# A macaron block of FFN, retention and FFN in fp32: how the first FFN prepares its weights and its x tiles, and in which order its engines work

## The chip, the core and the metric

The kernel runs on one core of a Trainium2 chip, in one launch. The metric is the device time of that launch in microseconds (us). The engines are called as in the profile: PE is TensorE, PEld its weight loads, DVE VectorE, ACT ScalarE, POOL GpSimd, SP the engine that only issues transfers (SPq).

## The reference

x has 1024 rows of 256 values, all in fp32. Both FFNs have the same weights.

```python
def ffn(x):      # scales are per output column; w_fp8 = w.astype(float8_e4m3fn).astype(float32)
    gate = silu((x @ gate_w_fp8) * gate_scale)          # 256 -> 768
    up = (x @ up_w_fp8) * up_scale                      # 256 -> 768
    return ((gate * up) @ down_w_fp8) * down_scale      # 768 -> 256
x = x + 0.5 * ffn(layernorm(x))
x = x + attn(layernorm(x))   # 16 heads of 16, rotated q and k, decay mask, group norm, silu gate, projection
x = x + 0.5 * ffn(layernorm(x))
```

## The kernel before

The rows of x are 8 tiles of 128 (NT), in two groups of four (NG, TH). Nothing is scheduled by a tool: each engine has a list of calls written out by hand, and executes it strictly in that order; semaphores with counts tie the lists together. A call that waits holds up all that stands behind it in its own list.

**Weights.** The first FFN rounds them to the fp8 grid itself. They come in eight pieces (PIECES): gate and up columns 0 to 127 (pieces 0, 1), 128 to 383 (2, 3), 384 to 767 (4, 5), and two halves of down (6, 7), with 256, 512, 768, 768 values a partition. For each piece DVE does `grid_step` (L574, exponent bits out of the raw weights), `grid_clip` (L580) and `grid_add` (L586, raw weight plus grid value); then the grid value is subtracted again, which leaves the rounded weight: `subtract`, on POOL (L293) for the pieces in SUB_ON_POOL, on DVE (L592) for the others. ACT copies the result twice: `to_half` (L385) to fp16 with a scale, `to_weights` (L391) to the fp32r tile that PE reads.

**x tiles.** For each tile `tile_stats` (L603) and `mean_var` (L607) on DVE, `roots` on POOL (L300, L302: 1/sqrt of the variances of a whole group of tiles), `norm_tile` on DVE (L632). PE turns each tile (`turn_h`, L961) into the banks of `turn`; when all four tiles of a group are turned, ACT copies the high halves (`split_h`, L398) and DVE takes the rest (`rest_h`, L644). So every product is done with a high and a low half.

**Products.** PRODUCTS lists twelve pairs (g, i) of the first FFN: group g, 128 columns i. `gate_up(j)` (L986) is 8 matmuls of 512 columns: gate high, gate low, up high, up low, two each. ACT does `silu` (L408), DVE `fuse_up` (L660), ACT `split_f` (L416), and the rest of it, `rest_f`, is on POOL (L308) for REST_ON_POOL, on DVE (L668) for the others. Product j shares its two banks with j-2. `down` (L1014) makes one x tile out of six column blocks; `scale_down` (L678) on DVE and `add_down` on POOL (L314) or, in the second FFN, on DVE (L683), add it to x. `turn_h2` (L1030) hands the first tile to the attention part.

**PE's filler.** WARM_UP matmuls on zeros (L1170) stand at the start, and `keep_busy` (L943) calls between the first steps.

**Transfers.** SP issues all of them, in the order gate piece 0, x tiles 0 to 3, up piece 1, gate piece 2, the masks, four small rows, x tiles 4 to 7, up piece 3, pieces 4 to 7, and then what later parts need.

## Time and profile before

| | us |
|---|---|
| median of 3 runs | 173.49 (173.36 to 173.67) |
| the profiled execution, its own time | 173.6 |
| its span, first to last instruction | 171.8 |
| PE busy | 161.0 (94%) |
| DVE busy | 137.1 (80%) |
| ACT busy | 75.9 (44%) |
| POOL busy | 68.9 (40%) |

PE is busy in 94% of the span, by a model that lets pipelined matmuls overlap, and it also counts the matmuls on zeros. Between the span and the time of the execution lie 1.8 us outside the instructions. The granted clock of TensorE is given as 0.999.

### The profile page before, as it was taken

The numbers are of one execution on the slowest core, as the hardware profiler recorded it, in microseconds if no ns is written. First come the engines' busy times: TensorE is split into PE (matmuls) and PEld (weight loads), VectorE is DVE, ScalarE is ACT, GpSimd is POOL, SyncE is SP. The second block draws the span as 40 slices with busy tenths as digits, with TensorE's granted clock in tenths as the row PEclk, the third lists the DMA queues.
The fourth block names the chain that finished last, engine by engine and source line by source line (L and its number), as shares of the span: only waits on it lengthen the run. The fifth ranks groups of instructions, "written<-read, shape, count | busy, mean of one in ns | idle before, by whom it ended". The sixth has DMA issues, their size and how long they took to land.

```text
span 171.8 us, 3264 instructions
## 1 busy us (share of the span) xinstructions
PE 161.0 (94%) x1125; PEld 123.1 (72%) x1125; DVE 137.1 (80%) x294; ACT 75.9 (44%) x162; POOL 68.9 (40%) x76
## 2 busy tenths in 40 slices
PE   5996998989989999999999999999899999999992
PEld 2454766678969786768686777867666788898881
DVE  2799989999847266869797979998887899666763
ACT  3145398869402306161707062534716646225600
POOL 2354295425580611117474746465297530000000
PEclk9999999999999999999999999999999999999999
DMA  4999203803000000000000000000000000011002
GB/s 155 277 352 310 84 2 64 306 0 120 4 0 0 4 0 0 4 0 0 6 0 4 2 0 0 4 0 6 0 0 2 0 4 0 0 61 61 6 31 92
DMA packets 6848, 8.41 MB, mean 49 GB/s; under 512 B 416, under 2 KB 5552, under 8 KB 6832
## 3 DMA queue, kind: packets, MB, share of 16 engines
q1 hardware_dynamic: 6832, 8.20, 14.9%
q8 instruction: 9, 0.15, 0.4%
q14 instruction: 7, 0.06, 0.1%
HBM read 7.15 MB, written 1.05 MB: 48 GB/s over the span
## 4 chain that ended last, share of the span: by engine, by line
PE 62%; DVE 19%; issue 7%; POOL 6%; DMA 3%; ACT 2%; SPq 0%; POOLq 0%; DVEq 0%
PE bank L986 18%; PE bank L1014 10%; PE bank L1042 7%; PE bank L1107 5%; POOL grstd L324 3%; PE bank L1053 3%; PE bank L1085 3%; PE bank L1056 3%; PE bank L1163 3%; DVE h L632 3%; DMA xt<-in_L_attn_x 3%; PE bank L1068 2%; DVE fuse L660 2%; DVE sc L715 2%; DVE grid L574 2%
## 5 line engine op out<-in xcount | busy, mean ns | idle before, releaser
L986 PE MATMUL bank<-hh,gate_r 128*128 128x512 f32 x96 | 27.6, 407 | 2.5 <-DVE hh L644 1.0
L986 PE MATMUL bank<-hh,up_r 128*128 128x512 f32 x96 | 26.3, 396 | 0.0
L1014 PE MATMUL bank<-down_r,fhi 128*128 128x256 f32 x96 | 24.3, 291 | 0.3 <-DVE flo L668 0.3
L324 POOL TENSOR_TENSOR grstd<-gve,neg_half 128x16 f32<-128x16 f32 x8 | 23.3, 2917 | 0.7
L1014 PE MATMUL bank<-down_r,flo 128*128 128x256 f32 x96 | 23.4, 282 | 0.0
L408 ACT ACTIVATE gact<-bank,vec 128x512 f32<-128x512 f32 x24 | 16.4, 685 | 14.9 <-PE bank L986 14.6
L986 PEld LDWEIGHTS bank<-hh,gate_r 128*128 128x128 f32 x96 | 16.8, 188 | 8.0 <-issue 3.7
L660 DVE SCALAR_TENSOR_TENSOR fuse<-bank,vec,gact 128x512 f32<-128x512 f32 x24 | 17.9, 745 | 4.1 <-PE bank L986 3.9
L986 PEld LDWEIGHTS bank<-hh,up_r 128*128 128x128 f32 x96 | 18.1, 188 | 4.3
L715 DVE TENSOR_TENSOR sc<-bank,msk 128x512 f32<-128x512 f32 x32 | 19.8, 680 | 0.0
L433 ACT ACTIVATE v<-bank 128x256 f32<-128x256 f32 x8 | 3.1, 384 | 37.0 <-PE bank L1056 37.0
L1014 PEld LDWEIGHTS bank<-down_r,fhi 128*128 128x128 f32 x96 | 18.1, 188 | 1.5 <-DVE flo L668 1.0
L1014 PEld LDWEIGHTS bank<-down_r,flo 128*128 128x128 f32 x96 | 18.1, 188 | 0.5 <-issue 0.2
L416 ACT ACTIVATE fhi<-fuse 128x512 fp32r<-128x512 f32 x24 | 14.9, 629 | 6.8 <-DVE fuse L660 6.8
L1042 PE MATMUL bank<-wqkv,h 128*128 128x512 f32 x32 | 15.1, 594 | 0.0
L668 DVE TENSOR_TENSOR flo<-fuse,fhi 128x512 fp32r<-128x512 f32 x18 | 13.3, 744 | 0.8 <-ACT fhi L416 0.7
L678 DVE TENSOR_TENSOR yd<-bank,ds 128x256 f32<-128x256 f32 x16 | 6.7, 422 | 8.5 <-PE bank L1014 8.4
L1107 PE MATMUL bank<-sc,v 128*32 128x128 f32 x256 | 13.1, 279 | 0.0
L300 POOL TENSOR_SCALAR ve<-mv 128x1 f32<-128x1 f32 (+3 forms) x14 | 3.8, 272 | 23.0 <-DVE mv L607 22.9
L293 POOL TENSOR_TENSOR grid<-raw,grid 128x256 f32<-128x256 f32 (+2 forms) x6 | 7.7, 1290 | 12.3 <-DVE raw L586 12.3
L308 POOL TENSOR_TENSOR flo<-fuse,fhi 128x512 fp32r<-128x512 f32 x6 | 9.6, 1611 | 4.9 <-ACT fhi L416 4.9
L302 POOL TENSOR_TENSOR rstd<-ve,neg_half 128x1 f32<-128x1 f32 (+3 forms) x14 | 10.0, 715 | 1.2
(80 smaller groups left out, 300.0 us busy)
## 6 DMA issues: line engine op xcount, KB each, us to landing
raw<-in_rotation SPq DMA_DIRECT2D x1, 1536.0 KB, 7.1
xt<-in_L_attn_x SPq DMA_DIRECT2D x2, 512.0 KB, 5.4
out<-xt SPq DMA_DIRECT2D x8, 128.0 KB, 1.7
raw<-in_L_ffn_down_w SPq DMA_DIRECT2D x2, 384.0 KB, 8.2
wqkv<-in_L_attn_w_qkv SPq DMA_DIRECT2D x1, 768.0 KB, 9.6
raw<-in_rotation SPq DMA_DIRECT2D x1, 512.0 KB, 3.5
raw<-in_L_ffn_gate_w SPq DMA_DIRECT2D x1, 384.0 KB, 7.2
raw<-in_L_ffn_up_w SPq DMA_DIRECT2D x1, 384.0 KB, 7.7
```

The lines of the kernel that those rows point to most:

```text
L302: pool.tensor_tensor(rstd[:, a:b], ve[:, a:b], neg_half[:, 0:b - a], ALU.pow).then_inc(rstd_done, 1)
L308: pool.tensor_tensor(flo[:, g % NG, i, :], fuse[:, j % FUSE_SLOTS, :], fhi[:, g % NG, i, :].bitcast(F32), ALU.subtract).then_inc(flo_pool, 1)
L324: pool.tensor_tensor(grstd[:, c % 2], gve[:, :], neg_half[:, :], ALU.pow).then_inc(grstd_done, 1)
L408: nc.scalar.activation(gact[:, j % 2, :], pairs[j // (NG * NI)][j % 2][0][:, :], ACT.Silu, scale=gate_col[:, i:i + 1]).then_inc(silu_done, 1)
L416: nc.scalar.activation(fhi[:, g % NG, i, :], fuse[:, j % FUSE_SLOTS, :], ACT.Copy).then_inc(fhi_done, 1)
L660: dve.scalar_tensor_tensor(out=fuse[:, j % FUSE_SLOTS, :], in0=pairs[j // (NG * NI)][j % 2][1][:, :], scalar=up_col[:, i:i + 1], in1=gact[ ...
L668: dve.tensor_tensor(flo[:, g % NG, i, :], fuse[:, j % FUSE_SLOTS, :], fhi[:, g % NG, i, :].bitcast(F32), ALU.subtract).then_inc(flo_dve, 1)
L715: dve.tensor_tensor(sc[:, r].rearrange("p k m t -> p (k m) t"), b_sc[r][:, :].rearrange("p (g t) -> p g t", t=P), causal.unsqueeze(1).to_b ...
L986: mm = pe.matmul(dst[:, :], wr[m][:, k * I + i * P:k * I + (i + 1) * P], half[:, k, g % NG, :], start=(k == 0 and half is hhi), stop=(k == ...
L1014: mm = pe.matmul(downs[d][:, 0:C], half[:, g % NG, i, t * P:(t + 1) * P], wr["down"][:, i * C:(i + 1) * C], start=(i == 0 and half is fhi) ...
L1042: mm = pe.matmul(b_qk[:, :], h2[:, c % 2, k, :], wqkv[:, k, 0:2 * C], start=(k == 0), stop=(k == KC - 1))
L1107: mm = pe.matmul(b_y[r * 2 * D:(r + 1) * 2 * D, k * P:(k + 1) * P], v2[:, c % 2, hd, :], sc[:, r, k, m, :], start=(c == 0 and m == 0), sto ...
```

## The change

Weights: there is one ACT pass instead of two (`to_weights` reads the grid tile in fp32, with the scale), the fp16 tile is gone, and the grid tile has three slots instead of two. The scale of the grid (LIFT) goes into `grid_clip` as a second operation, and `grid_add` becomes a plain addition. The new scales of h, of the weights and of the fused product cancel in the vectors and in `half_scale`.

x: it comes in three transfers (tiles 0 and 1, 2 and 3, 4 to 7), the first one ahead of all others. The roots of the first FFN are taken in three groups (0, 1), (2, 3), (4 to 7). Tiles 0, 2, 4 and 6 are normalised by ACT (`norm_act`), which needs a small DVE operation per group (`shift_rows`), tiles 1, 3, 5 and 7 by DVE as before.

PE: the first product does both high halves before both low halves (`first_gate_up`); the gate parts of products 1 and 2 come ahead of `turn_h(1)`, the up parts behind it; in `gate_up` the gate part waits for one thing (the silu of j-2) and the up part for the other (the fuse of j-2), in both FFNs. WARM_UP goes from 5 to 3, the `keep_busy` calls from 9 to 4. The last `down` calls of the second FFN stand in another order: the last two column blocks come only after the first four of tiles 4 to 6, and tile 7 is done whole at the end.

The lists of all engines in the first FFN are new, the sharing of `subtract` and `rest_f` between DVE and POOL too. The diff, cut to its core (indented less; lists as far as they change):

```diff
-GRID = 2.0 ** -20
+LIFT = 2.0 ** 20
 GRID_MIN = 1.5 * 2.0 ** -6
-W_SCALE = 144.0
+W_SCALE = 1.125 * 2.0 ** 119
+H_SCALE = 2.0 ** -90
+F_SCALE = 2.0 ** -60
+GRID_SLOTS = 3
+X_ROOTS = 3
...
-SUB_ON_POOL = [0, 1, 2, 3, 4, 6]
+SUB_ON_POOL = [1, 2, 3, 4, 5, 7]
...
-REST_ON_POOL = [0, 1, 2, 6, 8, 11]
+REST_ON_POOL = [0, 1, 2, 4, 11]
 FUSE_SLOTS = 4
-WARM_UP = 5
+WARM_UP = 3
...
+def normed_until(n):
+    return (n + 1) // 2 if n < NT else n + 1 - NT // 2
...
+        root_groups = ([(0, 2), (2, TH), (TH, NT)] + [(n, n + 1) for n in range(NT, 2 * NT)]
...
+sp.dma_start(xt[:, 0:2, :], x_dram[0][:, 0:2, :]).then_inc(x_in[0], 16)
 load_piece(0)
-sp.dma_start(xt[:, 0:TH, :], x_dram[0]).then_inc(x_in[0], 16)
+sp.dma_start(xt[:, 2:TH, :], x_dram[0][:, 2:TH, :]).then_inc(x_in[1], 16)
 load_piece(1)
-load_piece(2)
 sp.dma_start(msk[:, :], mask_t).then_inc(mask_in, 16)
 for src, at, n in ((gate_s, 0, NI), (up_s, NI, NI), (gn_w, 2 * NI, KC), (gn_b, 2 * NI + KC, KC)):
     sp.dma_start(rows[at:at + n, :], src.rearrange("(i p) -> i p", p=P)).then_inc(rows_in, 16)
-sp.dma_start(xt[:, TH:NT, :], x_dram[1]).then_inc(x_in[1], 16)
-for q in range(3, len(PIECES)):
+load_piece(2)
+load_piece(3)
+sp.dma_start(xt[:, TH:NT, :], x_dram[1]).then_inc(x_in[2], 16)
+for q in range(4, len(PIECES)):
     load_piece(q)
...
 pool.wait_ge(const_done, 1)
-subtract(0)
 roots(0)
-for n in range(1, 4):
-    subtract(n)
 roots(1)
+subtract(1)
+subtract(2)
+subtract(3)
+roots(2)
 subtract(4)
-for n in range(0, 3):
-    rest_f(n)
-subtract(6)
-rest_f(6)
-rest_f(8)
+rest_f(0)
+subtract(5)
+rest_f(1)
+rest_f(2)
+rest_f(4)
+subtract(7)
 add_down(0)
+roots(X_ROOTS)
 add_down(1)
-rest_f(11)
+roots(X_ROOTS + 1)
 add_down(2)
 add_down(3)
-roots(3)
-roots(4)
-for n in range(4, 8):
-    add_down(n)
+rest_f(11)
+roots(X_ROOTS + 2)
+add_down(4)
+add_down(5)
+add_down(6)
+add_down(7)
...
-def to_half(q):
+def to_weights(q):
     if q in SUB_ON_POOL:
         act.wait_ge(sub_pool, subs(q + 1)[1])
     else:
         act.wait_ge(sub_dve, subs(q + 1)[0])
-    if q >= 2:
-        act.wait_ge(w_ready, q - 1)
-    nc.scalar.activation(packed(w16, q), packed(grid, q), ACT.Copy,
-                         scale=W_SCALE / GRID).then_inc(half_done, 1)
-def to_weights(q):
-    act.wait_ge(half_done, q + 1)
-    nc.scalar.activation(piece(wr[PIECES[q][0]][:, :], q), packed(w16, q), ACT.Copy).then_inc(w_ready, 1)
+    nc.scalar.activation(piece(wr[PIECES[q][0]][:, :], q), packed(grid, q), ACT.Copy,
+                         scale=W_SCALE).then_inc(w_ready, 1)
+def norm_act(n):
+    act.wait_ge(shift_done, roots_until(n))
+    if n >= TH:
+        act.wait_ge(turned, n - TH + 1)
+    nc.scalar.activation(h[:, n % TH, :], xt[:, n, :], ACT.Identity, scale=rstd[:, n:n + 1],
+                         bias=shift[:, n:n + 1]).then_inc(h_act, 1)
...
+    nc.scalar.activation(hhi[:, k, g % NG, :], turn[g][k][:, :], ACT.Copy, scale=H_SCALE).then_inc(hhi_done, 1)
...
 nc.scalar.activation(warm[:, :], neg_half[:, 0:1], ACT.Silu)
-to_half(0)
+norm_act(0)
 to_weights(0)
-to_half(1)
-to_weights(1)
-to_half(2)
+norm_act(2)
 split_h(0, 0)
 split_h(0, 1)
+to_weights(1)
 to_weights(2)
-to_half(3)
+silu(0)
 to_weights(3)
-silu(0)
+norm_act(4)
+norm_act(6)
 silu(1)
 split_h(1, 0)
 split_h(1, 1)
 split_f(0)
 silu(2)
+to_weights(4)
+silu(3)
+silu(4)
 split_f(1)
-to_half(4)
-silu(3)
-to_weights(4)
 split_f(2)
-to_half(5)
-silu(4)
+split_f(3)
 to_weights(5)
 silu(5)
-split_f(3)
+silu(6)
 split_f(4)
-silu(6)
 split_f(5)
-to_half(6)
 silu(7)
 to_weights(6)
+split_f(6)
+split_f(7)
 silu(8)
-for n in range(6, 9):
-    split_f(n)
 silu(9)
-to_half(7)
+split_f(8)
 to_weights(7)
 silu(10)
 split_f(9)
+silu(11)
+copy_h2(0)
 split_f(10)
-silu(11)
 split_f(11)
-copy_h2(0)
-copy_v(0)
 copy_h2(1)
 copy_qk(0)
+copy_v(0)
 for c in range(NT - 1):
...
     dve.wait_ge(raw_in[q], 16)
-    if q >= 2:
-        dve.wait_ge(half_done, q - 1)
+    if q >= GRID_SLOTS:
+        dve.wait_ge(w_ready, q - GRID_SLOTS + 1)
...
-    dve.tensor_scalar(packed(grid, q), packed(grid, q), GRID_MIN, None, ALU.max).then_inc(clip_done, 1)
+    dve.tensor_scalar(packed(grid, q), packed(grid, q), GRID_MIN, LIFT, ALU.max, ALU.mult).then_inc(clip_done, 1)
-    dve.scalar_tensor_tensor(out=w, in0=w, scalar=GRID, in1=packed(grid, q),
-                             op0=ALU.mult, op1=ALU.add).then_inc(added, 1)
+    dve.tensor_tensor(w, w, packed(grid, q), ALU.add).then_inc(added, 1)
...
+def shift_rows(g):
+    a, b = root_groups[g]
+    dve.wait_ge(rstd_done, g + 1)
+    dve.scalar_tensor_tensor(out=shift[:, a:b], in0=mv[:, a:b, 0], scalar=-1.0, in1=rstd[:, a:b],
+                             op0=ALU.mult, op1=ALU.mult).then_inc(shift_done, 1)
...
-    dve.tensor_scalar(vec[:, 0:2 * NI], bank[7][:, 0:2 * NI], 1.0 / W_SCALE, None, ALU.mult).then_inc(vec_done, 1)
+    dve.tensor_scalar(vec[:, 0:NI], bank[7][:, 0:NI], 1.0 / (W_SCALE * H_SCALE), None,
+                      ALU.mult).then_inc(vec_done, 1)
+    dve.tensor_scalar(vec[:, NI:2 * NI], bank[7][:, NI:2 * NI], F_SCALE / (W_SCALE * H_SCALE), None,
+                      ALU.mult).then_inc(vec_done, 1)
...
-    dve.tensor_tensor(hlo[:, k, g % NG, :], turn[g][k][:, :], hhi[:, k, g % NG, :].bitcast(F32),
-                      ALU.subtract).then_inc(hlo_done, 1)
+    dve.scalar_tensor_tensor(out=hlo[:, k, g % NG, :], in0=turn[g][k][:, :], scalar=H_SCALE,
+                             in1=hhi[:, k, g % NG, :].bitcast(F32), op0=ALU.mult,
+                             op1=ALU.subtract).then_inc(hlo_done, 1)
...
+tile_stats(0)
 grid_step(0)
-grid_clip(0)
-grid_add(0)
-tile_stats(0)
 tile_stats(1)
 mean_var(0)
+grid_clip(0)
+mean_var(1)
+grid_add(0)
 tile_stats(2)
-mean_var(1)
 tile_stats(3)
+grid_step(1)
 mean_var(2)
-grid_step(1)
 mean_var(3)
+shift_rows(0)
+grid_clip(1)
+norm_tile(1)
+subtract(0)
 grid_step(2)
-grid_clip(1)
+norm_tile(3)
 grid_clip(2)
+grid_step(3)
+shift_rows(1)
+grid_clip(3)
 grid_add(1)
 grid_add(2)
-for n in range(0, 4):
-    norm_tile(n)
+grid_add(3)
+rest_h(0, 0)
 tile_stats(4)
+rest_h(0, 1)
+mean_var(4)
+tile_stats(5)
+tile_stats(6)
+tile_stats(7)
+mean_var(5)
+mean_var(6)
+mean_var(7)
 turned_vectors()
-mean_var(4)
-grid_step(3)
-tile_stats(5)
-grid_clip(3)
-rest_h(0, 0)
-grid_add(3)
-tile_stats(6)
-mean_var(5)
-tile_stats(7)
-mean_var(6)
 grid_step(4)
-mean_var(7)
-rest_h(0, 1)
+grid_step(5)
 grid_clip(4)
-grid_step(5)
-for n in range(4, 8):
-    norm_tile(n)
+shift_rows(2)
+norm_tile(5)
+norm_tile(7)
+grid_add(4)
+grid_clip(5)
 fuse_up(0)
-grid_clip(5)
-grid_add(4)
 rest_h(1, 0)
+rest_h(1, 1)
 fuse_up(1)
-rest_h(1, 1)
+fuse_up(2)
+grid_step(6)
 grid_add(5)
-fuse_up(2)
-subtract(5)
+grid_clip(6)
 fuse_up(3)
-grid_step(6)
-half_scale()
-grid_clip(6)
 fuse_up(4)
 grid_add(6)
+rest_f(3)
 fuse_up(5)
+subtract(6)
+fuse_up(6)
+fuse_up(7)
 grid_step(7)
-rest_f(3)
-fuse_up(6)
 grid_clip(7)
-rest_f(4)
+grid_add(7)
 rest_f(5)
-fuse_up(7)
-grid_add(7)
 fuse_up(8)
-subtract(7)
+rest_f(6)
 rest_f(7)
+rest_f(8)
+half_scale()
+scale_down(0)
 fuse_up(9)
 fuse_up(10)
+tile_stats(NT)
+scale_down(1)
 rest_f(9)
-scale_down(0)
+mean_var(NT)
+scale_down(2)
+norm_tile(NT)
+tile_stats(NT + 1)
+mean_var(NT + 1)
+scale_down(3)
+norm_tile(NT + 1)
+fuse_up(11)
 rest_f(10)
-scale_down(1)
-tile_stats(8)
-fuse_up(11)
-mean_var(8)
-tile_stats(9)
-scale_down(2)
-mean_var(9)
-norm_tile(8)
-scale_down(3)
+tile_stats(NT + 2)
+mean_var(NT + 2)
 rotate_parts(0)
-norm_tile(9)
 rotate(0)
-tile_stats(NT + 2)
...
     for t in range(TH):
-        if g == 0 and t == 1:
+        if g == 0 and t >= 2:
             keep_busy(1)
-        pe.wait_ge(h_done, n0 + t + 1)
+        if g < NG and t % 2 == 0:
+            pe.wait_ge(h_act, g * TH // 2 + t // 2 + 1)
+        else:
+            pe.wait_ge(h_done, normed_until(n0 + t))
         for k in range(KC):
             mm = pe.transpose(turn[g][k][:, t * P:(t + 1) * P], h[:, (n0 + t) % TH, k * P:(k + 1) * P], ident)
         mm.then_inc(turned, 1)
+def first_gate_up():
+    pe.wait_ge(hhi_done, KC)
+    for half in (hhi, hlo):
+        if half is hlo:
+            pe.wait_ge(hlo_done, KC)
+        for m in ("gate", "up"):
+            pe.wait_ge(w_ready, 1 if m == "gate" else PIECES_NEEDED[0])
+            for k in range(KC):
+                mm = pe.matmul(pairs[0][0][m == "up"][:, :], wr[m][:, k * I:k * I + P], half[:, k, 0, :],
+                               start=(k == 0 and half is hhi), stop=(k == KC - 1 and half is hlo))
+            if half is hlo:
+                mm.then_inc(gate_done if m == "gate" else up_done, 1)
 def gate_up(j, parts=("gate", "up")):
...
-    if g < NG:
-        pe.wait_ge(w_ready, PIECES_NEEDED[i])
     if i == 0:
         pe.wait_ge(hhi_done, KC * (g + 1))
-    if j >= 2:
-        pe.wait_ge(silu_done, j - 1)
-        pe.wait_ge(fuse_done, j - 1)
     if j == NG * NI:
         pe.wait_ge(hlo_done, KC * (NG + 1))
     elif j == NG * NI + 1:
         pe.wait_ge(sc_masked, HG * NT)
     for m in parts:
+        if g < NG:
+            pe.wait_ge(w_ready, PIECES_NEEDED[i] - (m == "gate"))
+        if j >= 2:
+            pe.wait_ge(silu_done if m == "gate" else fuse_done, j - 1)
         dst = pairs[g // NG][j % 2][m == "up"]
...
-gate_up(0)
+first_gate_up()
+gate_up(1, ("gate",))
+gate_up(2, ("gate",))
 turn_h(1)
-for j in range(1, 9):
+gate_up(1, ("up",))
+gate_up(2, ("up",))
+for j in range(3, 9):
     gate_up(j)
...
-down(d, 0, NI - 2)
-for d in range(NT + TH + 1, 2 * NT):
+for d in range(NT + TH, 2 * NT - 1):
     down(d, 0, NI - 2)
-    down(d - 1, NI - 2)
-down(2 * NT - 1, NI - 2)
+for d in range(NT + TH, 2 * NT - 1):
+    down(d, NI - 2)
+down(2 * NT - 1)
```

## Rows read from the trace of the kernel before

**Rows 1.** Busy time by stage: us, each engine's busy us (instructions), PEclk, DMA share, GB/s.

```profile
0.00:9.06 9.06, 7.29 (x11) 2.91 (x11) 4.53 (x17) 2.32 (x4) 3.36 (x9) 1.00 0.73 224
9.06:17.18 8.12, 6.32 (x31) 4.39 (x30) 8.12 (x22) 4.14 (x8) 3.83 (x6) 1.00 0.99 328
17.18:48.97 31.79, 30.11 (x150) 23.67 (x151) 30.46 (x47) 21.71 (x35) 16.99 (x14) 1.00 0.25 78
48.97:132.38 83.41, 81.88 (x735) 61.94 (x736) 65.39 (x152) 31.79 (x90) 40.44 (x46) 1.00 0.01 2
```

**Rows 2.** The chain that ended last: start us, us, what (three of its pieces).

```profile
1.20 4.32 DMA xt<-in_L_attn_x
...
16.55 0.59 DVE hh L644
...
132.38 1.88 PE bank L986 x8
```

**Rows 3.** Timeline of PE at the handover to the attention part.

```profile
48.97 0.44 PE L1030 MATMUL bank<-msk,h 128*128 128x128 f32 x2 [0.58 <-DVE h L632]
```

**Rows 4.** Timeline of the transfers' issue by SP.

```profile
4.59 0.39 SPq L268 DMA_DIRECT2D xt<-in_L_attn_x  x1
5.02 0.51 SPq L259 DMA_DIRECT2D raw<-in_L_ffn_up_w  x1
```

**Rows 5.** DMA issues by line: KB, us from issue to landing.

```profile
raw<-in_L_ffn_up_w SPq DMA_DIRECT2D x1, 256.0 KB, 6.7
```

**Rows 6.** Instructions by form until 48.97: busy us, mean ns, idle before.

```profile
L660 DVE SCALAR_TENSOR_TENSOR fuse<-bank,vec,gact 128x512 f32<-128x512 f32 x12 | 8.9, 740 | 0.1
...
L603 DVE BATCH_NORM_STATS2 stats<-xt 128x6 f32<-128x256 f32 x8 | 3.2, 409 | 1.4 <-DMA xt<-in_L_attn_x 1.4
...
L644 DVE TENSOR_TENSOR hh<-bank,hh 128x512 fp32r<-128x512 f32 x4 | 2.7, 676 | 0.7 <-ACT hh L398 0.7
...
L586 DVE SCALAR_TENSOR_TENSOR raw<-raw,grid 128x512 f32<-128x512 f32 x2 | 1.4, 680 | 0.0
...
L385 ACT ACTIVATE w<-grid 128x256 f16<-128x256 f32 x2 | 0.8, 416 | 6.8 <-POOL grid L293 6.8
```

**Rows 7.** Timeline of DVE and POOL where the two meet.

```profile
26.09 1.37 DVE L592 TENSOR_TENSOR grid<-raw,grid 128x768 f32<-128x768 f32 x1
...
26.98 1.64 POOL L308 TENSOR_TENSOR flo<-fuse,fhi 128x512 fp32r<-128x512 f32 x1 [0.33 <-ACT fhi L416]
...
47.48 1.28 POOL L308 TENSOR_TENSOR flo<-fuse,fhi 128x512 fp32r<-128x512 f32 x1
...
47.55 1.36 DVE L632 TENSOR_SCALAR h<-x,mv,rstd 128x256 f32<-128x256 f32 x1
```

**Rows 8.** Timeline of DVE: the fuse of products 0 and 2.

```profile
19.43 0.74 DVE L660 SCALAR_TENSOR_TENSOR fuse<-bank,vec,gact 128x512 f32<-128x512 f32 x1
...
25.43 0.74 DVE L660 SCALAR_TENSOR_TENSOR fuse<-bank,vec,gact 128x512 f32<-128x512 f32 x1
```

**Rows 9.** Timeline of the weight loads of PE's matmuls on zeros.

```profile
6.20 0.34 PEld L1170 LDWEIGHTS bank<-v 128*128 128x128 f32 x1 [0.52 <-issue]
7.05 0.34 PEld L1170 LDWEIGHTS bank<-v 128*128 128x128 f32 x1 [0.52 <-issue]
7.68 0.19 PEld L1170 LDWEIGHTS bank<-v 128*128 128x128 f32 x1 [0.29 <-issue]
8.11 0.19 PEld L1170 LDWEIGHTS bank<-v 128*128 128x128 f32 x1 [0.24 <-issue]
```

**Rows 10.** Timeline of PE, then of DVE, at the end of the kernel.

```profile
163.78 0.28 PE L1014 MATMUL bank<-down_r,flo 128*128 128x256 f32 x1
164.40 0.38 PE L1014 MATMUL bank<-down_r,fhi 128*128 128x256 f32 x1 [0.34 <-DVE flo L668]
...
168.17 0.28 PE L1014 MATMUL bank<-down_r,flo 128*128 128x256 f32 x1
...
168.82 0.41 DVE L678 TENSOR_TENSOR yd<-bank,ds 128x256 f32<-128x256 f32 x1
```

More of the change, by code:

```diff
@@ L125, in macaron @@
         raw = sb("raw", [P, 3 * KC * I])
-        grid = sb("grid", [P, 2, KC * 384])
-        w16 = sb("w16", [P, 2, KC * 384], F16)
+        grid = sb("grid", [P, GRID_SLOTS, KC * 384])
+        shift = sb("shift", [P, NT])
         wr = {m: sb(f"{m}_r", [P, KC * I], F32R) for m in ("gate", "up", "down")}
@@ L207, in macaron @@
         b_gn = [bank[7]] * (NT - 2) + [bank[6], bank[0]]
-        x_in = [sem(f"x_in{g}") for g in range(NG)]
+        x_in = [sem(f"x_in{n}") for n in range(3)]
         mask_in, rows_in, ds_in = sem("mask_in"), sem("rows_in"), sem("ds_in")
@@ L235, in macaron @@
             sem(n) for n in ("gn_turned", "ga_done", "go_done", "proj_done", "x2_done"))
-        root_groups = ([(g * TH, (g + 1) * TH) for g in range(NG)] + [(n, n + 1) for n in range(NT, 2 * NT)]
+        root_groups = ([(0, 2), (2, TH), (TH, NT)] + [(n, n + 1) for n in range(NT, 2 * NT)]
                        + [(2 * NT, 2 * NT + TH - 1), (2 * NT + TH - 1, 2 * NT + TH), (2 * NT + TH, 3 * NT - 2),
@@ L981, in gate_up @@
                         if half is hlo:
-                            if j == 0 and m == "gate":
-                                keep_busy(4)
                             pe.wait_ge(hlo_done, KC * (g + 1))
```

36 lines of the change are left out of this document (16 added, 20 removed).

## The prediction, made before the changed kernel was run

> **What bounds the kernel now.** I read four views in this order. The busy times by stage [rows 1] show where PE has idle time that can be won: before 17.18 it has hardly a product to do, from 17.18 to 48.97 it is busy 30.1 of 31.8 us, and from there to 132.38 in 81.9 of 83.4. DVE is as full in the first FFN: 8.12 of 8.12 us from 9.06 on, 30.5 of 31.8 after that. So two engines are full there, and the question is when the first product can start and which of the two then holds the rest. The chain of waits [rows 2] gives the answer for the start: x lands at 5.52 (1.20 plus 4.32), and all from there to the first product is DVE work, which ends with the low half of the first four tiles at 17.14 (16.55 plus 0.59). The timeline then shows the handover [rows 3]: `turn_h2(0)` starts at 48.97 and PE had waited 0.58 us for the normalised tile. The last view is the end of the kernel [rows 10].
>
> The profiled execution took 173.6 us for a span of 171.8; the median of the runs shown is 173.49. The sum is made against 173.6, and the difference is taken over to the median. Within 0.2% (0.35 us) a measurement of this kernel can't tell a change from none.
>
> **Step A, the start, until both low halves of the first group are there (17.14 now).** Tiles 2 and 3 still land behind 640 KB, so about 5.5. DVE now has only tiles 1 and 3 to normalise. ACT's `norm_act` has no row; its nearest is a 256-wide ACT pass from SBUF, 416 ns [rows 6]; I bound it by that and by twice that, and take 0.42, plus a small DVE operation a group (under 0.2).
>
> What sets the time is a queue: `norm_act(2)` needs `shift_rows(1)`, and that stands on DVE behind `grid_step(3)`, which waits for piece 3. Piece 3 is issued in its old slot at about 5.0, from where it took 6.7 us, to 11.7 [rows 4, 5]. The 512 KB of x tiles 4 to 7, which were issued just ahead of it, now come behind; at the 328 GB/s of that stretch [rows 1] they are 1.6 us, which gives 10.1. From below it is no wait at all: DVE gets to `grid_step(3)` at about 9.1, as behind 5.5 its list has ten operations of 256 values (0.4 each, as the statistics' 409 ns) less 0.8 of overlap between neighbours and 0.4 of short ones more. Between the two I take 9.5: DVE loses 0.4 there.
>
> From 9.5: `grid_step` and `shift_rows` 0.55, `norm_act(2)` with its hop 0.5, four transposes and one `keep_busy` 1.05, two `split_h` 1.1: ACT is done at 12.7. DVE meanwhile does `grid_clip(3)` and three `grid_add` (680 ns at 512 values [rows 6], 0.4 at 256), with one POOL `subtract` of 0.7 between them (see step C), also until 12.7. Then `rest_h` twice with one `tile_stats` between, 1.7 [rows 6]: 14.4. `rest_h` is now a scalar_tensor_tensor out of PSUM like the fuse, 740 ns against 676 [rows 6], 0.06 more each, 0.5 for all eight and on the path only here, in these 1.7. **Gain 2.7** (17.14 to 14.4; 2.1 with piece 3 at 10.1, 3.1 with no wait for it).
>
> **Step B, to the end of the fuse of product 2 (25.43 plus 0.74, so 26.17 now) [rows 8].** DVE goes on without a stop, at durations as in [rows 6] and for other widths in proportion: the rest of the statistics of tiles 4 to 7 (three of 0.4, four short ones) 1.6, vectors and three 768-wide grid operations of 0.5 1.9, `shift_rows(2)` and two `norm_tile` 0.9, `grid_add(4)` and `grid_clip(5)` 1.4, fuse 0 0.7, `rest_h` twice 1.3, fuses 1 and 2 1.3: 9.1 less 0.5 of overlap between neighbours, 8.6, against 9.03 now. It ends at 23.0. PE would be ready: product 2's up part can follow fuse 0, which ends at 20.3, where it ended at 20.17 before [rows 8]. So fuse 0 gains nothing, and fuse 2 gains **3.2**, because the second group's transposes and the gate parts of 1 and 2 are already done by then.
>
> **Step C, to the first normalised tile of the attention part (47.55 plus 1.36, 48.91 now) [rows 7].** A DVE operation with two SBUF inputs, or a one-input one from SBUF, and a POOL operation on SBUF take turns here, whole operations at a time: the DVE subtraction at 26.09 takes 1.37 us beside a POOL `rest_f`, the POOL one at 26.98 then 1.64 instead of 1.28, and `norm_tile(8)` 1.36 beside the POOL one at 47.48 [rows 7]. Products out of PSUM don't take part. In this stretch DVE loses `subtract(5)`, `subtract(7)` (1.4 each, with their waits), `rest_f(4)` 0.65 and the 0.95 of waiting in `norm_tile(8)`, and gets `subtract(6)` 0.9, `rest_f(6)` and `(8)` 1.3, `grid_add(5)` from the stretch before 0.9, and a new wait of 0.55 for POOL's `add_down(1)`, behind which `norm_tile(8)` comes: 4.4 less, 3.65 more, so 22.0 instead of 22.7. End at 45.0, **gain 3.9**. PE as a check: 14.4 plus the 30.1 us that it was busy [rows 1] is 44.5, so it is nearly full and no more than 0.5 better would be had. Every one of some ten hops between engines that I set at zero costs 0.05 or so; I take 0.4 off: **3.5**.
>
> ACT loses eight passes and gets four short ones; it had 10 us to spare from 17.18 on [rows 1], and nothing is priced for it. `rest_f(11)` moves behind `add_down(3)` on POOL and ends near 49.8, when down(4)'s second part wants it at 50.0; that cover is thin, and 0.3 would be lost if it were gone. `copy_v(0)` goes behind `copy_qk(0)`, but its first reader on PE stands two projections later. `subtract(7)` precedes the late rotation table; it ends near 37, before 40.05, where that was issued. From 48.97 to 132.38 PE is busy in 98% [rows 1], with the same list, so what is won is passed on.
>
> **Step D, the end.** Four matmuls of the last blocks stood behind a wait for the last low half: from 163.78 to 164.40 are 0.62 instead of 0.12, so 0.5 of gap [rows 10]. With eight more matmuls of tile 6 in front of it the gap closes. Tile 7 ended 0.47 after tile 6 and its first DVE operation came at 168.82 although PE ended at 168.45 (168.17 plus 0.28) [rows 10]: it stood behind tile 6. Now twelve matmuls lie between, and it starts right behind PE, at 167.95. **Gain 0.85** (0.5 if the queue on DVE stays). The split waits in `gate_up` are nothing there, as PE hardly waits in the second FFN.
>
> **Sum.** 3.5 + 0.85 = 4.35: 169.25 for the profiled execution, 169.15 for the median; I say 169.2. Its own range: piece 3 0.5 either way, hops and turns 0.7, end 0.3: 168.1 to 170.4.
>
> **Rivals.**
> (1) *The transfer holds the start.* If piece 3 lands only at 11.0, when x tiles 4 to 7 did, step A gains 1.2 instead of 2.7: 170.7. For it: the slot is the same, and this transfer took 6.7 us in it [rows 5]. Against: 512 KB less lie ahead of it.
> (2) *The other side: TensorE is at its lower level when the products begin.* Three warm-up calls end at 6.9, before that rise, and then PE has, by my times, one stretch of 2 us with nothing (8.5 to 10.5) and 4 fillers instead of 9. A product is 1.88 us [rows 2], so each product at the lower level costs 1.9: one 171.1, two 172.9, and from the third on (5.6 against 4.35) the kernel is slower than before, 174.8. Against: the gate part's first matmuls wait for DVE anyway, and work, though thin, never ends. The Trainium skill (TensorE: Matmul & The Clock Gate, Part 1) says that the half clock is the idle state, that sustained work lifts it and idling brings it back. By that rule a cut of the fillers is a risk, not a saving; no row here shows PE fall back.
> (3) *The lists give it back.* POOL and DVE take turns, and each lost turn is a POOL operation of 1.28 [rows 7]. Two more on DVE's path in steps B and C, or fuse 5 held by `rest_f(1)`, which now stands behind `subtract(5)` on POOL: 171.7. DVE is full, so nothing absorbs it.
> (4) *Better*: hops cost nothing and piece 3 is early, PE becomes the bound, 4.4, and starts 0.4 sooner: with the 0.85 that is 5.65, 167.8 or below.
>
> **Chances.** Forecast 0.57; rival 1 0.10; rival 2 0.16, of it 0.05 with three products or more; rival 3 0.10; rival 4 0.05; something else, near no change, 0.02. The range 167.9 to 171.6 takes in the forecast, rival 1, one product of rival 2 and half of rival 3, about 0.8. Faster 0.92, same 0.03, slower 0.05.
>
> **What would show it.** In the profile after: `grid_step(3)` starting at 9.5 with a wait for the transfer before it (A); the first low product at 14.4 and fuse 2 ending near 23 (B); `turn_h2(0)` near 45.4 (C); no gap in PE after the last product and a last tile 0.85 nearer to it (D). Wrong would be: loads of the first products 0.4 apart instead of 0.2, a wait on POOL in front of fuse 5 over 1 us, or a handover later than 46.5.

## The result, and the profile after

The changed kernel takes 168.52 us (median of 4, 168.31 to 169.21) beside 173.43 for the kernel before: ratio 0.9738, 95% interval 0.9709 to 0.9766. Run again later, it took 168.84 (168.03 to 170.03), ratio 0.9764, 0.9708 to 0.9821. The forecast was 169.2, in a range of 167.9 to 171.6. The profiled execution took 168.31 us for a span of 166.5, so 5.3 less than the 173.6 of before. By the medians the gain is 4.9: the profiled execution of before is one of the slower ones of its kernel, that of after the fastest of its four. The ratios leave out an execution that took over 1.5% longer than the fastest one of the same kernel.

Busy time by stage, after, cut where the cuts of before answer [rows 1]:

```profile
0.00:9.06 9.06, 6.90 (x13) 2.82 (x13) 4.65 (x19) 2.50 (x4) 3.74 (x10) 1.00 0.69 211
9.06:13.75 4.69, 3.06 (x14) 2.08 (x14) 4.69 (x11) 2.41 (x5) 3.25 (x3) 1.00 1.02 347
13.75:44.78 31.03, 29.26 (x152) 23.61 (x151) 28.13 (x54) 19.07 (x32) 18.75 (x14) 1.00 0.37 118
44.78:128.01 83.23, 81.70 (x735) 61.74 (x734) 67.45 (x155) 33.00 (x92) 42.05 (x47) 1.00 0.01 1
```

The second stage took 8.12 us and takes 4.69; DVE is full in it as before, it merely has less to do. The third went from 31.79 to 31.03, the fourth is as it was. The chain that ended last shows what each stretch hangs on (start us, us, what):

```profile
1.72 3.92 DMA xt<-in_L_attn_x
...
7.18 1.33 POOL rstd L314
...
10.08 2.07 DVE raw L600 x3
...
15.11 1.08 POOL ve L312
...
16.26 1.25 POOL rstd L314
...
18.48 1.06 PE bank L992 x8
...
20.50 4.90 PE bank L1028 x20
...
27.22 1.24 DVE flo L692
...
38.39 1.69 PE bank L1056 x12
40.08 1.86 PE bank L1028 x8
41.93 2.85 PE bank L1056 x24
44.78 0.22 PE bank L1072 x2
```

Up to 20.5 it still runs through DVE and POOL, then it changes between PE and DVE. From 38.39 to the handover it is PE alone: `turn_h2(0)` stood behind a wait of 0.58 us for the normalised tile [rows 3], and now it stands only behind PE's own work. DVE's timeline from the third transfer to the fuse of product 2, which answers [rows 6, 8]:

```profile
8.04 0.43 DVE L588 TENSOR_SCALAR grid<-raw 128x512 uint32<-128x512 uint32 x1 [0.37 <-DMA raw<-in_L_ffn_gate_w]
...
9.20 0.42 DVE L588 TENSOR_SCALAR grid<-raw 128x512 uint32<-128x512 uint32 x1
...
10.00 2.16 DVE L600 TENSOR_TENSOR raw<-raw,grid 128x256 f32<-128x256 f32 x3
12.14 0.69 DVE L667 SCALAR_TENSOR_TENSOR hh<-bank,hh 128x512 fp32r<-128x512 f32 x1
...
13.08 0.67 DVE L667 SCALAR_TENSOR_TENSOR hh<-bank,hh 128x512 fp32r<-128x512 f32 x1
...
15.12 1.02 DVE L588 TENSOR_SCALAR grid<-raw 128x768 uint32<-128x768 uint32 x2
...
17.54 0.16 DVE L612 SCALAR_TENSOR_TENSOR shift<-mv,rstd 128x4 f32<-128x4 f32 x1 [0.93 <-POOL rstd L314]
...
19.61 0.74 DVE L684 SCALAR_TENSOR_TENSOR fuse<-bank,vec,gact 128x512 f32<-128x512 f32 x1
20.27 1.28 DVE L667 SCALAR_TENSOR_TENSOR hh<-bank,hh 128x512 fp32r<-128x512 f32 x2
21.47 1.40 DVE L684 SCALAR_TENSOR_TENSOR fuse<-bank,vec,gact 128x512 f32<-128x512 f32 x2
```

`grid_step(3)` (9.20) waits for nothing. The low halves are there at 13.75, fuse 2 ends at 22.87 (21.47 plus 1.40). Two waits stand here that the forecast did not have: 0.37 us for gate piece 2 (8.04), and 0.93 us for the roots of the second group (17.54).

| | before | after | gain so far | forecast |
|---|---|---|---|---|
| low halves of the first group | 17.14 | 13.75 | 3.4 | 2.7 |
| end of fuse 2 | 26.17 | 22.87 | 3.3 | 3.2 |
| handover to the attention part | 48.97 | 44.62 | 4.35 | 3.5 |
| first product of the second FFN | 132.38 | 128.01 | 4.4 | 3.5 |
| end of the span | 171.8 | 166.5 | 5.3 | 4.35 |

### The profile page after: what moved, and what is told of

It reads as the page before. It is cut to its first block, busy times and chain, and to the rows that moved or that the text cites. A ratio compares the mean times of both kernels' runs of the same rounds, so it can differ in the third digit from the quotient of the medians.

```text
span 166.5 us, 3227 instructions
## 1 busy us (share of the span) xinstructions
PE 156.1 (94%) x1111; PEld 120.4 (72%) x1111; DVE 133.4 (80%) x295; ACT 72.9 (44%) x158; POOL 72.1 (43%) x77
## 4 chain that ended last, share of the span: by engine, by line
PE 63%; DVE 18%; POOL 7%; issue 6%; DMA 2%; ACT 1%; SPq 1%; DVEq 0%; POOLq 0%
PE bank L1028 17%; PE bank L1056 12%; PE bank L1084 7%; PE bank L1149 5%; POOL grstd L336 4%; PE bank L1095 3%; PE bank L1127 3%; PE bank L1098 3%; PE bank L1205 3%; DVE flo L692 3%; PE bank L1110 2%; DMA xt<-in_L_attn_x 2%; DVE raw L600 2%; DVE sc L739 2%; DVE fuse L684 2%
## 5 line engine op out<-in xcount | busy, mean ns | idle before, releaser
L1028 PE MATMUL bank<-hh,gate_r 128*128 128x512 f32 x92 | 25.8, 402 | 0.1
L1028 PE MATMUL bank<-hh,up_r 128*128 128x512 f32 x92 | 25.4, 397 | 0.0
L1028 PEld LDWEIGHTS bank<-hh,up_r 128*128 128x128 f32 x92 | 17.0, 188 | 4.5 <-issue 0.8
L433 ACT ACTIVATE fhi<-fuse 128x512 fp32r<-128x512 f32 x24 | 14.8, 626 | 8.7 <-DVE fuse L684 8.7
L692 DVE TENSOR_TENSOR flo<-fuse,fhi 128x512 fp32r<-128x512 f32 x19 | 14.9, 793 | 0.8 <-ACT fhi L433 0.7
L312 POOL TENSOR_SCALAR ve<-mv 128x1 f32<-128x1 f32 (+3 forms) x15 | 4.7, 313 | 21.8 <-DVE mv L627 21.6
L305 POOL TENSOR_TENSOR grid<-raw,grid 128x768 f32<-128x768 f32 (+2 forms) x6 | 10.5, 1763 | 7.7 <-DVE raw L600 7.7
L314 POOL TENSOR_TENSOR rstd<-ve,neg_half 128x1 f32<-128x1 f32 (+3 forms) x15 | 11.1, 738 | 1.3
L1149 PEld LDWEIGHTS bank<-sc,v 128*32 128x32 f32 x256 | 8.3, 109 | 2.6 <-DVE sc L739 0.7
```

Source lines behind the costliest of these rows:

```text
L305: pool.tensor_tensor(packed(grid, q), piece(raws[PIECES[q][0]], q), packed(grid, q), ALU.subtract).then_inc(sub_pool, 1)
L314: pool.tensor_tensor(rstd[:, a:b], ve[:, a:b], neg_half[:, 0:b - a], ALU.pow).then_inc(rstd_done, 1)
L433: nc.scalar.activation(fhi[:, g % NG, i, :], fuse[:, j % FUSE_SLOTS, :], ACT.Copy).then_inc(fhi_done, 1)
L692: dve.tensor_tensor(flo[:, g % NG, i, :], fuse[:, j % FUSE_SLOTS, :], fhi[:, g % NG, i, :].bitcast(F32), ALU.subtract).then_inc(flo_dve, 1)
L1028: mm = pe.matmul(dst[:, :], wr[m][:, k * I + i * P:k * I + (i + 1) * P], half[:, k, g % NG, :], start=(k == 0 and half is hhi), stop=(k == ...
L1149: mm = pe.matmul(b_y[r * 2 * D:(r + 1) * 2 * D, k * P:(k + 1) * P], v2[:, c % 2, hd, :], sc[:, r, k, m, :], start=(c == 0 and m == 0), sto ...
```

## The experiments

In all tables "handover" is the start of the first `turn_h2` matmul in the profiled execution (44.62 in the timeline after; the chain and the stage cut have it at 44.78, where the matmul before it ends), and "times" are all executions of the kernel.

### The end of the kernel, both ways

The order of the last `down` calls alone, undone in the changed kernel and done alone in the kernel before (its inverse):

```diff
-for d in range(NT + TH, 2 * NT - 1):
+d = NT + TH
+down(d, 0, NI - 2)
+for d in range(NT + TH + 1, 2 * NT):
     down(d, 0, NI - 2)
-for d in range(NT + TH, 2 * NT - 1):
-    down(d, NI - 2)
-down(2 * NT - 1)
+    down(d - 1, NI - 2)
+down(2 * NT - 1, NI - 2)
```

> The changed kernel with the last down calls in their old order. If step D is right (the gap in PE of 0.5 us comes back, and tile 7 again stands behind tile 6 on DVE), the time is 0.85 to 0.9 us above the changed kernel's 168.5: 169.4. Rival: only the gap of PE counts, 169.0.

> The kernel before with the new order of the last down calls and nothing else. Step D alone: 0.85 to 0.9 us below 173.4, so 172.5. Rival: the order saves only together with the new waits in gate_up, 173.0 to 173.4.

The kernel before with the new order: 172.13 us against 173.17, ratio 0.9949 (0.9932 to 0.9965), which is 0.6 to 1.2 us. The changed kernel with the old order: 169.83, ratio 0.9801 (0.9763 to 0.9839), 1.3 later than 168.52; three of its four executions had a mean granted clock of 0.986 or less, so that size is not the tail's alone. The traces give it without the start: from the first product of the second FFN to the end of the span are 38.5 us in the changed kernel (128.01 to 166.5) and 39.4 with the old order (127.49 to 166.9), 39.4 in the kernel before (132.38 to 171.8) and 38.6 with the new one (131.64 to 170.2). So the order is worth 0.9 us in both kernels. PE's timeline shows the gap back where it was [rows 10]:

```profile
159.51 0.39 PE L1056 MATMUL bank<-down_r,fhi 128*128 128x256 f32 x1 [0.34 <-DVE flo L692]
```

and in the trace of after the last matmul and the last DVE operations are

```profile
163.20 0.28 PE L1056 MATMUL bank<-down_r,flo 128*128 128x256 f32 x1
...
163.53 0.42 DVE L702 TENSOR_TENSOR yd<-bank,ds 128x256 f32<-128x256 f32 x1
163.99 0.42 DVE L707 TENSOR_TENSOR xt<-yd,x 128x256 f32<-128x256 f32 x1
```

DVE starts on the last tile 0.05 behind PE's end (163.48), where it stood 0.37 behind it [rows 10]. Step D's 0.85 is shown.

### The split waits

Both waits of `gate_up` ahead of the gate part again, all else as changed:

```diff
+if j >= 2:
+    pe.wait_ge(silu_done, j - 1)
+    pe.wait_ge(fuse_done, j - 1)
 ...
-    if j >= 2:
-        pe.wait_ge(silu_done if m == "gate" else fuse_done, j - 1)
```

> The changed kernel, but in gate_up both waits (silu and fuse of j-2) stand ahead of the gate part again. The gate part of product 2 then waits for fuse 0 (ends 20.3), and the second group's transposes behind it, so that they start 2 us later than their 18.5: if the steps B and C are right and PE and DVE are both full there, 1.5 to 2 us are lost, 170.0 to 170.5. Rival: DVE holds that stretch anyway and the loss is under 0.5, 169.0.

Measured: 175.75 us (174.58 to 176.94), ratio 1.0151 (1.0098 to 1.0204): slower than the kernel before, 7.2 later than changed. PE's timeline, then its busy time by stretches (columns as in [rows 1]):

```profile
19.82 1.50 PE L1029 MATMUL bank<-hh,gate_r 128*128 128x512 f32 x4 [4.52 <-issue]
21.11 1.91 PE L992 MATMUL bank<-msk,h 128*128 128x128 f32 x8
22.67 2.64 PE L1029 MATMUL bank<-hh,up_r 128*128 128x512 f32 x8
```

```profile
15.00:20.00 5.00, 0.48 (x3) 0.21 (x2) 3.79 (x9) 2.48 (x5) 3.12 (x3) 1.00 0.72 261
20.00:24.00 4.00, 4.00 (x15) 3.38 (x15) 0.31 (x1) 0.94 (x2) 0.73 (x1) 0.57 0.00 1
```

Gate part 2 stands ahead of `turn_h(1)`, and with the joint wait it needs fuse 0, which ends on DVE at 19.71 (18.97 plus 0.74). So PE stands for 4.52 us, the second group is turned after that, and DVE has 0.31 us of work in the next four. In those four the granted clock is 0.57: the eight transposes take 1.91 us instead of 1.06. From the first low half on DVE (11.50, and 12.14 in the trace of after) to the handover (50.87 and 44.62) this kernel needs 6.9 us more; from there to the end of the span both need 121.9, so in the second FFN the split waits are worth nothing. The loss is the stall and the fallen clock together; the runs do not separate them. The new place of the gate parts and the split waits are one edit; the first without the second loses more than the whole change brings.

### The turn ahead of the gate parts

```diff
-gate_up(1, ("gate",))
-gate_up(2, ("gate",))
 turn_h(1)
-gate_up(1, ("up",))
-gate_up(2, ("up",))
-for j in range(3, 9):
+for j in range(1, 9):
```

> The changed kernel with turn_h(1) directly behind the first product and products 1 and 2 whole behind it. PE then idles from the first product's end (about 15) to the tiles at 18.4, and the 8 gate matmuls (1.9 us) come after it: if PE's order is worth what step B says, 1 to 1.9 us are lost, 169.5 to 170.4. Rival: DVE sets the pace, below 0.4 lost, 168.5 to 168.9.

Measured: 169.98, 170.69, 172.86 and 173.07 us, mean clocks 0.988, 0.987, 0.978 and 0.978; ratio 0.9838 (0.9808 to 0.9868) from the two fastest. The trace of the fastest, busy time by stretches, then PE's timeline:

```profile
8.00:10.00 2.00, 0.42 (x2) 0.02 (x1) 1.93 (x7) 0.58 (x1) 0.20 (x1) 1.00 0.90 255
10.00:14.00 4.00, 3.93 (x13) 3.12 (x14) 3.50 (x8) 1.94 (x5) 3.81 (x3) 0.57 1.03 351
14.00:16.00 2.00, 1.54 (x7) 0.92 (x5) 2.00 (x12) 0.55 (x1) 0.90 (x2) 1.00 0.90 258
```

```profile
18.69 1.07 PE L992 MATMUL bank<-msk,h 128*128 128x128 f32 x8 [3.15 <-ACT h L407]
```

PE had waited 1.65 us for tile 2, the second one that ACT normalises, and then the clock fell, at a place that the edit does not touch: it only moves work behind 14.8. In the trace of after PE waited 1.69 us at the same place and the clock stayed at 1.00:

```profile
10.38 0.44 PE L992 MATMUL bank<-msk,h 128*128 128x128 f32 x2 [1.69 <-ACT h L407]
```

So the same cover of PE holds the clock in one execution and not in the next, and the four times mix that with the order of the turn. The trace separates the two. From 14.00 on the clock is at 1.00 again, and `turn_h(1)` starts at 18.69, only 0.21 us later than in the trace of after; but the handover comes at 46.32, 1.70 later. The order of the turn is worth the difference, 1.5 us. ACT's list has `silu(1)` ahead of the second group's high halves, so with the turn first they wait for product 1: DVE's `rest_h` of the second group starts at 21.93 instead of 20.27.

### The changed kernel once more, and with the old fillers

The changed kernel unaltered, and with `WARM_UP` 5 and the nine `keep_busy` calls of before:

```diff
-WARM_UP = 3
+WARM_UP = 5
 ...
-if g == 0 and t >= 2:
+if g == 0 and t == 1:
 ...
+    keep_busy(4)          # ahead of first_gate_up's low halves
 ...
+keep_busy(2)              # behind the warm-up
```

> The changed kernel once more, unaltered, beside the next three on one chip. If the cause of its spread is the clock that is granted while TensorE's work is thin (mean clocks of 1.000, 0.999, 0.997 and 0.990 went with 168.31, 168.64, 168.41 and 169.21 us), the times lie at 168.3 to 168.6 where the mean clock is 0.997 or more and at 169.2 or later where it is 0.990 or less. If the spread has another cause, the times don't follow the mean clock. Median 168.5.

> The changed kernel with the fillers of the kernel before: the longer warm-up, two fillers ahead of tile 1's turn and four ahead of each turn of tiles 1 to 3, instead of one each ahead of tiles 2 and 3. Theory 1: the thin cover of the new start is what lets the clock fall in some executions, and the fillers run in time in which TensorE waits anyway (it is busy 0.62 of the 2 us from 9 to 11). Then the mean clock is 0.997 or more in every execution, the spread is under 0.4 us and the median 168.3 to 168.6. Theory 2: fillers that stand ahead of a late tile's transposes cost what they last, some 0.25 us each where the product before them ends late: up to 1 us ahead of tile 3, which gives 169.0 to 169.6 with a steady clock. Theory 3: fillers have no bearing on the clock; the spread stays as it is.

The edit is not quite what this expectation describes: it has two fillers ahead of the first turn, one ahead of tile 1's and four ahead of the low halves, as the kernel before, besides the two ahead of the first product that both kernels have.

| | times | mean clocks | handover |
|---|---|---|---|
| changed, first | 168.31, 168.64, 168.41, 169.21 | 1.000, 0.999, 0.997, 0.990 | 44.62 |
| changed, again | 170.03, 168.09, 169.59, 168.03 | 0.98, 1.00, 0.99, 1.00 | 46.35 |
| old fillers | 169.13, 168.20, 168.97, 167.80 | 0.998, 1.00, 1.00, 1.00 | 45.43 |

The profiled execution is the first of each row. The times of the changed kernel follow the clock: 168.03 to 168.64 at 0.997 or more, 169.21 to 170.03 at 0.990 or less. With the old fillers the clock holds, yet the times still spread over 1.3 us, so theory 1 on the fillers is only half right. The profiled executions show both causes side by side. In both of these gate piece 2 took 4.5 us to land instead of the 3.4 of after, and DVE started on it at 9.04 and 9.07 instead of 8.04. The changed kernel, again, PE (timeline) and DVE:

```profile
8.47 0.20 PE L1215 MATMUL bank<-msk,rows 16*128 16x16 f32 x1 [2.08 <-DMA rows<-in_L_attn_gn_bias]
...
9.04 0.43 DVE L588 TENSOR_SCALAR grid<-raw 128x512 uint32<-128x512 uint32 x1 [1.27 <-DMA raw<-in_L_ffn_gate_w]
...
13.85 0.69 DVE L667 SCALAR_TENSOR_TENSOR hh<-bank,hh 128x512 fp32r<-128x512 f32 x1 [0.86 <-ACT hh L415]
```

and by stretches:

```profile
8.00:9.00 1.00, 0.53 (x4) 0.53 (x5) 0.00 (x0) 0.22 (x1) 0.34 (x1) 0.90 0.84 261
9.00:15.00 6.00, 5.20 (x16) 3.76 (x15) 5.09 (x12) 2.38 (x5) 3.66 (x3) 0.50 1.06 348
15.00:16.00 1.00, 1.00 (x4) 0.76 (x4) 1.00 (x4) 0.13 (x1) 0.35 (x1) 0.68 1.03 392
```

With the old fillers, DVE, and by stretches:

```profile
9.07 0.43 DVE L588 TENSOR_SCALAR grid<-raw 128x512 uint32<-128x512 uint32 x1 [1.64 <-DMA raw<-in_L_ffn_gate_w]
...
12.94 0.68 DVE L667 SCALAR_TENSOR_TENSOR hh<-bank,hh 128x512 fp32r<-128x512 f32 x1
```

```profile
9.00:15.00 6.00, 5.09 (x27) 3.90 (x26) 5.93 (x15) 2.62 (x5) 3.64 (x3) 1.00 0.95 317
```

The first low half starts at 12.14 in the trace of after, at 12.94 here, at 13.85 there. The late transfer costs 0.80 us, and this kernel took 0.82 more (169.13 against 168.31). By this pair the clock costs another 0.91: the short warm-up ended at 6.40, the small rows came at 8.47 and PE stood for 2.08 us; the changed kernel took 0.90 more again (170.03). That DVE waits 0.86 us for ACT's high half is the mark of it: ACT waits for transposes and fillers at the lower level.

### The transfers

x in two transfers and the old order on SP, all else as changed:

```diff
-sp.dma_start(xt[:, 0:2, :], x_dram[0][:, 0:2, :]).then_inc(x_in[0], 16)
 load_piece(0)
-sp.dma_start(xt[:, 2:TH, :], x_dram[0][:, 2:TH, :]).then_inc(x_in[1], 16)
+sp.dma_start(xt[:, 0:TH, :], x_dram[0]).then_inc(x_in[0], 16)
 load_piece(1)
+load_piece(2)
 ...
-load_piece(2)
-load_piece(3)
-sp.dma_start(xt[:, TH:NT, :], x_dram[1]).then_inc(x_in[2], 16)
-for q in range(4, len(PIECES)):
+sp.dma_start(xt[:, TH:NT, :], x_dram[1]).then_inc(x_in[1], 16)
+for q in range(3, len(PIECES)):
```

> The changed kernel with the old transfers: x in two parts, first gate piece first, gate piece 2 ahead of the masks. Tiles 2 and 3 land no later than now, tiles 0 and 1 two us later (5.5 for 3.55), so their statistics and the first grid operations, about 1.2 us of DVE, come behind 5.5 and the whole chain of DVE up to the low halves moves by 1.0 to 1.3: 169.5 to 169.8. Rival: the first transfer only fills time in which DVE waits for tiles 2 and 3 anyway, under 0.4: 168.9.

Measured: 170.99 us (170.65 to 171.49), ratio 0.9885 (0.9859 to 0.9910), mean clock 0.98 in every execution. DVE's timeline:

```profile
10.61 0.43 DVE L586 TENSOR_SCALAR grid<-raw 128x512 uint32<-128x512 uint32 x1 [0.97 <-DMA raw<-in_L_ffn_up_w]
```

Up piece 3, issued at 5.03 behind x tiles 4 to 7, took 5.56 us and landed at 10.59; issued ahead of them it landed at 8.7. So `grid_step(3)` came 1.41 later, 0.97 of it this wait and 0.44 the later x tiles, the first low half 2.29 later (14.43), the handover 2.31. The other 0.9 is again the clock, at 0.50 from 9 to 15. Here the fall goes with the edit, since all four executions have a mean clock of 0.98: between the end of the warm-up at 6.25 and the first normalised tile at 8.31 PE has one small transpose of 0.20 us.

### ScalarE's two parts

All tiles of the first FFN normalised on DVE:

```diff
-norm_act(0)
+norm_tile(0)      # and so for tiles 2, 4 and 6, in DVE's list
 ...
-shift_rows(0)     # and (1), (2)
```

> The changed kernel with all eight x tiles normalised on DVE and none on ACT. Four operations of 0.34 come back to DVE, less three small ones of 0.1; as DVE is full, 0.7 ahead of the first low halves and 0.7 ahead of the second group count: 169.2 to 169.9. Rival: an ACT pass (0.60) is longer than a DVE one (0.41), and the hop through shift_rows costs more, so it is no worse or better: 168.0 to 168.6.

Two ACT passes again per piece, the first to an fp32 tile:

```diff
+nc.scalar.activation(tmp, packed(grid, q), ACT.Copy).then_inc(half_done, 1)
+act.wait_ge(half_done, q + 1)
-nc.scalar.activation(piece(wr[PIECES[q][0]][:, :], q), packed(grid, q), ACT.Copy,
+nc.scalar.activation(piece(wr[PIECES[q][0]][:, :], q), tmp, ACT.Copy,
                      scale=W_SCALE).then_inc(w_ready, 1)
```

> The changed kernel with two ACT passes per weight piece again (through an fp32 tile, since fp16 can't hold the new range). Eight passes of 0.42 to 0.85, 5.5 us, come back to ACT, which has 10 us to spare. If ACT's one pass was worth nothing by itself, as step C has it: under 0.3, 168.5 to 168.8. Rival: a second pass stands in front of silu calls on whose result PE waits, and 0.8 or more is lost: 169.3 and above.

And in the kernel before, the second pass taken away; the weights then go from the grid tile straight to the tile that PE reads, without the rounding to fp16:

```diff
-nc.scalar.activation(packed(w16, q), packed(grid, q), ACT.Copy, scale=W_SCALE / GRID).then_inc(half_done, 1)
+nc.scalar.activation(piece(wr[PIECES[q][0]][:, :], q), packed(grid, q), ACT.Copy,
+                     scale=W_SCALE / GRID).then_inc(w_ready, 1)
```

> The kernel before with one ACT pass per weight piece straight from the fp32 grid tile (scale 144 over the grid, no fp16) and nothing else changed. By step C, nothing: 172.9 to 173.4, as DVE and PE are full and ACT is not. Rival: the weights of the third to sixth piece come 0.6 to 0.8 sooner and the chain runs over ACT's second pass now and then: 172.4.

| | us | ratio (interval) |
|---|---|---|
| all tiles on DVE | 169.05 (168.90 to 169.16) | 0.9770 (0.9755 to 0.9784) |
| two passes | 168.89 (168.46 to 170.26) | 0.9783 (0.9733 to 0.9833) |
| one pass, in the kernel before | 173.35, beside 173.06 | 1.0011 (0.9998 to 1.0024) |

One pass alone is worth nothing in the kernel before, and in the changed kernel the second pass costs nothing that stands out of the spread. The normalisation on ACT is worth 0.5 us by the medians, which is within the spread of the changed kernel; in the profiled executions, both at full clock, the first low half starts 0.2 later without it (12.36) and the handover 0.75 later (45.37). PE gets its third tile there after a wait of 0.49 us instead of 1.69, since tile 2 no longer stands behind `shift_rows(1)`:

```profile
8.95 0.44 PE L986 MATMUL bank<-msk,h 128*128 128x128 f32 x2 [0.49 <-DVE h L651]
```

### Fillers moved, and lists around the fourth tile

First kernel: four fillers ahead of tile 2's turn, none ahead of tile 3's, two ahead of `turn_h(1)`. Second kernel: two ahead of tile 2, and the lists changed (DVE's below; on POOL `roots(2)` stands ahead of `subtract(3)`, on ACT `norm_act(4)` and `(6)` ahead of `to_weights(3)`).

```diff
 # both kernels, PE
-if g == 0 and t >= 2:
-    keep_busy(1)
+if g == 0 and t == 2:
+    keep_busy(4)       # second kernel: 2
 ...
+keep_busy(2)
 turn_h(1)
 # second kernel, DVE
 grid_step(2)
+shift_rows(1)
 ...
 grid_step(3)
-shift_rows(1)
 ...
-grid_add(3)
 rest_h(0, 0)
 ...
 mean_var(7)
+grid_add(3)
```

> The changed kernel with its fillers at other places: four ahead of tile 2's turn, none ahead of tile 3's, two ahead of the turn of h of tile 1. The filler ahead of tile 3 stands in a stretch in which TensorE is nearly always busy (3.11 of 3.25 us from 13.75 to 17.0), so it costs its own length there. Theory 1: 0.2 to 0.5 us earlier than the changed kernel, 168.0 to 168.3, with mean clocks of 0.997 or more. Theory 2: the end of the start is set by VectorE (2.81 of 3.35 us from 17.0 to 20.35) and by the roots on GpSimd, not by TensorE; then the place of one filler is worth nothing, 168.4 to 168.6.

> The kernel with the moved fillers, and with lists changed around the fourth tile: tile 1's mask rows, the residual and the statistics go ahead of the third grid addition, GpSimd's roots of the first group ahead of its subtraction of tile 3, and ScalarE's normalisation of tiles 4 and 6 ahead of its pass over the last weights. In the changed kernel the roots took 1.07 and 1.24 us where VectorE's grid steps run beside them, VectorE waited 0.93 us for them at 17.54 and TensorE 1.23 us for h at 18.48. Theory 1: these waits are on the path, half to all of the 1.23 us comes back, 166.9 to 167.7. Theory 2: the wait is only moved, since the third grid addition holds the weights of tile 3 and VectorE has 2.81 us of work in 3.35 us there: 168.0 to 168.6. Theory 3: tile 3's product comes later by the 0.7 us of a grid addition and drags the group's handover with it: 169.0 or more.

| | times | mean clocks | ratio (interval) |
|---|---|---|---|
| fillers moved | 168.50, 168.61, 167.84, 168.37 | 1.000, 0.999, 1.000, 1.000 | 0.9729 (0.9706 to 0.9753) |
| and the lists | 171.09, 168.14, 168.38, 169.99 | 0.99, 1.00, 1.00, 0.99 | 0.9759 (0.9704 to 0.9814), without the first |

The fillers bring 168.44, where the eight executions of the changed kernel have a median of 168.5 and a mean of 168.8: no gain at full clock, as theory 2 had it, and no execution above 168.61. The lists bring nothing at full clock (168.14 and 168.38) and lose the clock in two of four. The timeline of the second kernel tells why, on DVE, POOL and PE:

```profile
17.17 1.22 DVE L612 SCALAR_TENSOR_TENSOR shift<-mv,rstd 128x4 f32<-128x4 f32 x1 [0.46 <-POOL rstd L314]
...
17.12 1.26 POOL L305 TENSOR_TENSOR grid<-raw,grid 128x512 f32<-128x512 f32 x1
...
19.17 1.06 PE L992 MATMUL bank<-msk,h 128*128 128x128 f32 x8 [2.34 <-ACT h L407]
```

The roots began 0.36 us earlier, but POOL then began the subtraction that was moved behind them, and DVE's `shift_rows(2)` on 128x4 values, 0.16 us in the changed kernel, took 1.22, nearly the length of the subtraction. PE stood 2.34 us for h instead of 1.23, and from 20 to 24 the granted clock of this trace is 0.57.

## Why the forecast held

**What bounds it** was read rightly: the start hangs on DVE, the rest on DVE and PE, and what is won goes through the attention part (4.35 at the handover, 4.4 at 128.01). By the medians the error is 0.7 us of a gain of 4.9, on the safe side; by the profiled pair 0.95 of 5.3.

**Step A** was given 2.7 and measured 3.4. The term that was too large is piece 3: forecast to be needed at 9.5 after a wait, it had landed at 8.7 and `grid_step(3)` started at 9.20. The bound from below (9.1, no wait) was the case, and the 328 GB/s that gave 10.1 were a poor guide to it; the run with the old transfers shows 10.59 for the old order, where 11.0 was rival 1's number. The clip and three additions behind it took 2.96 to 12.16 with the step, where the forecast had 3.2. `norm_act` was mis-sized the other way: 597 ns each, not 420. It does not show, as DVE was the later one. The sum is 0.3 + 0.24 + 0.1 for the two low halves. Part of the agreement is luck. The forecast watched piece 3; what held DVE was gate piece 2, with the 0.37 us before 8.04, for which it had no term, and in two other traces that wait is 1.27 and 1.64.

**Step B** came out (3.3 for 3.2), but by two errors that cancel: A ended 0.65 early, and the stretch from there took 9.12 us for the forecast's 8.6. "DVE goes on without a stop" is wrong: it waits 0.93 us for the second group's roots. POOL's `ve`, the first of the two operations of `roots`, took 1.07 us beside two DVE grid steps. In the kernel before the same operation took 0.23 beside a DVE operation out of PSUM. The trace of after, then that of before:

```profile
15.11 1.07 POOL L312 TENSOR_SCALAR ve<-mv 128x4 f32<-128x4 f32 x1 [0.55 <-DVE mv L627]
```

```profile
16.64 0.23 POOL L300 TENSOR_SCALAR ve<-mv 128x4 f32<-128x4 f32 x1 [0.59 <-DVE mv L607]
```

These 0.84 us are nearly the whole wait. The forecast had the rule that such operations take turns and applied it to long ones only. That a gain in A is lost again here is seen in the first two lines of the table: 3.4, then 3.3. That fuse 0 gains nothing held (20.17, forecast 20.3, measured 20.35). What the forecast left unpriced is how much hangs on the split waits: it gave them nothing in the second FFN, which stands, and took their use in the first for granted. There they are worth 6.9 us by the traces, 7.2 by the medians.

**Step C** was given 3.9 less 0.4 and measured 4.35 at PE (4.6 at `norm_tile(8)`, which ends at 44.33). The allowance of 0.4 for hops was not needed; it had no row. The stretch itself took 21.46 us (22.87 to 44.33) for the forecast's 22.0, though DVE lost a turn in it that the forecast had not priced (rival 3 below); which term made up for that was not worked out. The check against PE, 14.4 plus 30.1, named the real bound: PE is busy 29.26 of 31.03 us, and DVE waits for it:

```profile
39.40 0.42 DVE L702 TENSOR_TENSOR yd<-bank,ds 128x256 f32<-128x256 f32 x1 [0.86 <-PE bank L1056]
...
43.40 0.42 DVE L702 TENSOR_TENSOR yd<-bank,ds 128x256 f32<-128x256 f32 x1 [0.91 <-PE bank L1056]
43.74 0.59 DVE L655 TENSOR_SCALAR h<-x,mv,rstd 128x256 f32<-128x256 f32 x1
```

`norm_tile(8)`, 1.36 beside a POOL operation before [rows 7], takes 0.59. The ACT passes were priced at nothing, and both runs on them bear it out.

**Step D** was given 0.85; the traces give 0.9 in either kernel, the times of the kernel before with this edit alone 0.6 to 1.2.

**The rivals.** Rival 1 did not come, but its mechanism is real: with the old transfers it is the 1.4 us of `grid_step(3)`. Rival 2 was half right. The first products ran at the upper level in the profiled execution, and 0.2 us apart; but in the other profiled execution of the same kernel the granted clock goes to 0.50 after a gap, and it costs about 0.9 us, less than half of the 1.9 a product it was given, because what runs in that stretch is mostly transposes and fillers with DVE's work beside them. The Trainium skill (TensorE: Matmul & The Clock Gate, Part 1) has idling bring the clock back down; the runs here agree, with 0.50 behind the gap of 2.08 us and 0.57 behind that of 1.65. The forecast had drawn from it that a cut of the fillers is a risk; here that is about 1 us in some executions, and no loss against the kernel before. Rival 3 came in two places, for less than its price. One is DVE's `rest_f(3)`, which took 1.78 us beside a POOL `rest_f` and not 0.69 as at 34.19; it is on the chain, but the kernel before has such turns too [rows 7]:

```profile
27.14 1.78 DVE L692 TENSOR_TENSOR flo<-fuse,fhi 128x512 fp32r<-128x512 f32 x1
```

The other is the 0.93 us for the roots. It lies in the 1.77 us that PE still idles between 13.75 and 44.78, of which 1.23 are the wait for h ahead of `turn_h(1)`; the lists of the last kernel were to win it and did not. Rival 4, with a chance of 0.05, is the nearer account of the profiled pair: piece 3 was early, the allowance for hops was not needed, PE was the bound from 38.39 on, and of its 5.65 us 5.3 came. So the range held, while two of the values that the forecast put into its sum, 9.5 for piece 3 and 0.4 for the hops, were too high.

**How the 5.3 divide.** The end is 0.9, shown from both kernels. The transfers are 1.4 of the start by the trace of the run that undoes them. One pass on ACT is nothing. ACT's normalisation is 0.5 by the medians and 0.75 by the profiled pair. The gate parts ahead of `turn_h(1)` are 1.5 by the trace, and they need the split waits. That leaves under 1 us for the order of the lists on DVE, POOL and ACT. It was not run alone, and whether the parts add up is not shown.

**What stays open.** Why the same gap of 1.65 to 1.69 us ends in a fallen clock in one execution and not in another; in the profiled execution with two ACT passes PE waited even 1.98 us there, and the clock stayed at 1.00. That more fillers hold the clock (eight executions at 0.998 or more, against three of eight at 0.990 or less without) is supported by the pair of traces above and by the run with the old order at the end, whose start is that of the changed kernel and which had three more of four at 0.986 or less. The kernel with all tiles on DVE had four at 0.998 or more with the few fillers; there PE waited 0.49 us at the place where it waits 1.69 in the changed kernel, which fits the gap being what counts, with fillers as one way to shorten it. The kernel with the changed lists had more fillers and still two executions at 0.99, with a gap of 2.34 us further on. How long a gap is safe is not shown.

## What to carry to other kernels

Before a call is moved ahead in a hand-written list, look at what it waits for together with what it needs: the gate parts ahead of the turn gain (1.5 us) only because their wait was split, and lose 7 us otherwise. Cover for TensorE at a start whose transfers jitter by a microsecond should be sized for the late transfer, not for the profiled one; here such cover cost nothing that could be measured at full clock. Where the operations of two engines take turns, the small ones are hurt most: count them too, and keep a long operation of the other engine from starting just ahead of one.

## What was not expected of the hardware

- The transfer of 256 KB issued at 4.59 us landed after 3.4 us in one execution and 4.5 in two others of nearly the same kernel (3.0 to 3.6 in seven more of its variants), with nothing changed ahead of it, and in the one pair with a steady clock the whole kernel's time moved with it (0.82 us for 0.80).
- A POOL operation on 128x4 values took 0.23 us beside a DVE operation out of PSUM and 1.07 beside two DVE grid steps; a DVE operation on 128x4 values took 0.16 us by itself and 1.22 beside a POOL subtraction of 1.26.
- The granted clock, once fallen, stayed at 0.50 through six us in which PE was busy 5.20 (9.00 to 15.00, the changed kernel again).
